# Three reorderings of an already tuned block: a subtraction moved ahead in the prologue, input transposes moved into an output projection, the first two tiles of a layer interleaved

## The chip, the cores and the metric

The kernel runs on one core of one Trainium2 chip. The metric is the device time of one execution in microseconds (us), lower is better. Names used here: PE is TensorE (PEld its weight loads), DVE is VectorE, ACT is ScalarE, POOL is GpSimd, SP is the engine that issues the transfers.

## The reference, cut to what matters

The reference computes one block on `x` of shape (4, 1024, 256). Each half begins with a layer norm without learned weights, scaled and shifted per batch by a small modulation product:

```python
h = _layernorm(x, axis=-1) * (1 + ca) + sa
x = x + ga * _L0_attn_ref(h, Wq, bq, Wk, bk, Wv, bv, Wo, bo)   # 16 heads of 64, causal, tanh projections
h = _layernorm(x, axis=-1) * (1 + cb) + sb
x = x + gb * _L0_ffn_ref(h, ...)                                # two layers

# attention
q, k, v = (tanh(states @ W + bias), split into heads)
ctx = softmax(causal(q @ k.T / 8)) @ v
return jnp.tanh(ctx @ Wo + bo)

# each of the two layers of the second half
h = shift_token(x); q, k, v = split(h @ wqkv)        # 8 heads of 64
q, k = rotary(l2norm(q) * qs, l2norm(k) * ksc)
x = x + local_attention(q, k, v) @ wo                # window 128
h = layernorm(shift_token(x)) * lg + lb
a, g = split(h @ w1 + b1); x = x + (a * gelu(g)) @ w2 + b2
```

## The kernel before, in words

Every engine has its own program, written by hand as a list of calls, with semaphores between them. So the order in which an engine does its work is the order of the lines; an engine that waits holds up all that is queued behind the waiting instruction. Matrix products are made from high and low parts (`three_products`, L71 to L76): an operand is split into a rounded high part by ACT (`stream_hi`) and a remainder by DVE (`stream_lo`), and three products are added up in PSUM. A projection of 512 columns is six matmuls (two halves of the 256 inputs by three products).

**Attention phase.** It runs batch after batch (four), and in a batch over eight pairs of heads. The input of a batch is normalised by DVE (`statistics`, `shifts`, `normalise_chunk`), transposed by PE (`stream_T`), split by `stream_hi` and `stream_lo`, all in two chunks of 512 tokens. For batches 0 and 1 this happens in the prologue; for batches 2 and 3 it happens at the end of batch 0 and of batch 1, beside the output projection. The one power on POOL (`inverse_deviations`, L269) gives the standard deviations.

In the prologue, PE makes six projections of the first pair (`PROJ`: values of chunk 0, values of chunk 1, queries 0, keys 0, queries 1, keys 1). A projection of chunk c waits for `stream_lo(0, c)`. ACT turns each into a full and a high part (`tanh_full` L517, `tanh_hi` L522), DVE subtracts them (`split_projection` L295); `tanh_full(i)` waits for `split_projection(i - 2)`, since there are two stage buffers. ACT's list is: projections 0, 1, 2, `stream_hi(1, 0)`, projections 3, 4, `stream_hi(1, 1)`, projection 5. Meanwhile POOL splits the output weights `wo` (L274 a cast, L276 a subtraction, 2048 elements a partition each), which the output projections need only at the end of the batch.

At a batch's end the output projection is made of four accumulations (c, m), chunk c of tokens by half m of the outputs, each of 24 matmuls over the eight pairs of heads. ACT applies tanh (L608), DVE the gate (`gate_attended` L469), PE transposes back (`output_T` L727), DVE adds to the residual (`add_attended` L476). PE's next batch begins with `scores(..., 1)`. PE, ACT and DVE each wait at the loop's top, or before it, for `n_lo`, which counts the finished `stream_lo`. For the third batch's end (and the fourth's) there is no later input to prepare.

**Layer phase.** Each of the two layers goes over 32 tiles of 128 tokens in a loop that is software pipelined by hand, and then over eight chunks of the feed-forward part. Ahead of the loop stands a start that takes tiles 0 and 1 and the transposes of tile 2 through their first steps. For a tile these are: POOL copies it (`stage_tile` L1105) and puts one carried column into the operand (`carry_in`, `carry_out`), PE transposes it (`stream_T` L1590), ACT and DVE split it, PE projects values, queries and keys (`project`, in the order 2, 0, 1), ACT squares queries and keys (`squares` L1215), DVE sums them (`squared_norms` L1377, L1379), POOL takes two powers (L1110, L1114), DVE rotates (`rotate_q`, `normalise_keys`, `rotate_k`), POOL adds the two halves of the rotation (`add_rotated` L1118), and PE transposes the result (`qk_T` L1613), which ACT (`copy_queries`) and DVE (`copy_keys`) copy out of PSUM. `qk_T(..., 0)` writes the same PSUM bank as `stream_T`, `qk_T(..., 1)` the same as the value projection. `carry_in` of tile t waits in POOL's list behind the powers of the tile before.

## Time and profile before

| | us |
|---|---|
| median of 3 runs (lowest to highest) | 2591.67 (2588.89 to 2592.57) |
| the profiled execution, its time | 2589.23 |
| its span in the trace | 2587.4 |
| PE busy in the span | 2381.7 |
| DVE / ACT / POOL busy | 1919.3 / 1543.3 / 618.5 |

The span is what the trace covers; 1.8 us lie around it. The mean granted clock of TensorE is 0.966 of full speed. A busy share is an average over stages with different limits, so the stages that the change touches have to be read one by one: the prologue (0 to 54 us), the ends of batches 0 and 1 (about 263 to 303 and 506 to 546 us) and the starts of the two layers (about 1062 to 1101 and 1814 to 1848 us).

### The profile page before, as it was taken

How to read it: one execution, taken by the hardware profiler on the slowest of the kernel's cores; microseconds unless marked ns; L12 is line 12 of the kernel's file. 1: busy time of each engine (PE TensorE's matmuls, PEld its weight loads, DVE VectorE, ACT ScalarE, POOL GpSimd, SP SyncE). 2: the span in 40 equal slices, each digit the busy share in tenths (PEclk: the TensorE clock that was granted, in tenths of full speed). 3: DMA queues.
4: the chain of work that ended last, by engine and by line, in shares of the span. 5: the costliest groups of instructions: out<-in, count | busy, mean ns of one | idle time of the engine just before them, and what ended most of it. 6: DMA issues, size and time to landing. Idle time of an engine off the chain costs nothing. (4 is left out here: it accounts for less than half of the span.)

```text
span 2587.4 us, 65680 instructions
## 1 busy us (share of the span) xinstructions
PE 2381.7 (92%) x21336; PEld 1898.6 (73%) x21336; DVE 1919.3 (74%) x4552; ACT 1543.3 (60%) x3026; POOL 618.5 (24%) x711
## 2 busy tenths in 40 slices
PE   5999899999999995299999998999799999998995
PEld 4767667767777774288888886888588888886884
DVE  6999699879969994567777776666477777765666
ACT  4777477667747773266666665344366666664442
POOL 1000000000000000444444444212344444442222
PEclk8999999999999998599999999999899999998998
DMA  3100100010001003100000000100100000001003
GB/s 110 39 18 12 56 19 12 29 46 16 15 6 52 12 18 113 64 1 0 8 0 8 1 8 3 48 0 0 45 0 7 1 8 0 8 0 51 0 0 130
DMA packets 70204, 62.43 MB, mean 24 GB/s; under 512 B 3972, under 2 KB 67196, under 8 KB 69760
## 3 DMA queue, kind: packets, MB, share of 16 engines
q1 hardware_dynamic: 70144, 61.66, 7.5%
q8 instruction: 34, 0.56, 0.1%
q14 instruction: 26, 0.21, 0.0%
HBM read 49.05 MB, written 8.40 MB: 22 GB/s over the span
## 5 line engine op out<-in xcount | busy, mean ns | idle before, releaser
L511 ACT ACTIVATE at_p<-at_ps_s,at_shift 128x1024 f32<-128x1024 f32 (+3 forms) x384 | 336.1, 900 | 85.6 <-PE at_ps_s L680 48.8
L311 DVE TENSOR_TENSOR at_p_lo<-at_p,at_p_hi 128x1024 f16<-128x1024 f32 (+3 forms) x384 | 357.2, 951 | 5.5
L1228 ACT ACTIVATE ly_probs<-ly_masked,ly_small,ly_rq 128x256 f32<-128x256 f32 x512 | 302.2, 592 | 40.0 <-DVE ly_small L1421 40.0
L1640 PEld LDWEIGHTS ly_ps<-ly_values,ly_probs_T 128*128 128x128 f32 x2048 | 248.3, 191 | 48.7 <-issue 48.7
L1640 PE MATMUL ly_ps<-ly_values,ly_probs_T 128*128 x2048 | 269.5, 274 | 12.6 <-ACT ly_probs_T L1236 12.6
L1418 DVE CUSTOM_DVE_ANT_0 ly_masked<-ly_ps,ly_mask 128x256 f32<-128x256 f32 x520 | 199.7, 421 | 91.5 <-PE ly_ps L1621 90.9
L1236 ACT ACTIVATE ly_probs_T<-ly_ps 128x512 f32<-128x512 f32 x256 | 151.9, 594 | 178.8 <-PE ly_ps L1630 131.2
L1118 POOL TENSOR_TENSOR ly_rope_a<-ly_rope_a,ly_rope_t 128x512 f32<-128x512 f32 x132 | 169.2, 1282 | 304.1 <-DVE ly_rope_t L1391 304.1
L708 PE MATMUL at_ps_o<-at_v,at_p_hi 128*128 128x65 f16 x2304 | 237.7, 193 | 0.0
L709 PE MATMUL at_ps_o<-at_v,at_p_hi 128*128 128x64 f16 x2304 | 236.8, 194 | 0.0
L708 PEld LDWEIGHTS at_ps_o<-at_v,at_p_hi 128*128 128x128 f16 x2304 | 210.6, 96 | 34.5 <-issue 25.7
L710 PE MATMUL at_ps_o<-at_v,at_p_lo 128*128 128x65 f16 x2304 | 235.7, 192 | 0.0
L306 DVE CAST at_p_hi<-at_p 128x1024 f16<-128x1024 f32 (+3 forms) x384 | 206.7, 556 | 30.0 <-ACT at_p L511 21.4
L1377 DVE TENSOR_REDUCE ly_norm<-ly_sq 128x8 f32<-128x512 f32 x136 | 93.3, 686 | 174.3 <-ACT ly_sq L1215 172.8
L710 PEld LDWEIGHTS at_ps_o<-at_v,at_p_lo 128*128 128x128 f16 x2304 | 212.3, 99 | 0.0
L709 PEld LDWEIGHTS at_ps_o<-at_v,at_p_hi 128*128 128x128 f16 x2304 | 212.0, 97 | 0.0
L74 PE MATMUL ly_ps<-ly_a_hi,ly_operands 128*128 128x512 f32 x408 | 181.1, 444 | 14.0 <-DVE ly_operands L1370 7.8
L74 PE MATMUL at_ps_m<-at_hT,at_w_hi 128*128 128x512 f32 (+1 forms) x396 | 175.3, 443 | 14.6 <-DVE at_hT L361 11.0
L517 ACT ACTIVATE at_stage<-at_ps_m,at_bias 128x512 f32<-128x512 f32 x198 | 136.0, 687 | 87.3 <-PE at_ps_m L76 84.1
L75 PE MATMUL ly_ps<-ly_a_lo,ly_operands 128*128 128x512 f32 x408 | 164.7, 404 | 0.0
L76 PE MATMUL ly_ps<-ly_a_hi,ly_operands 128*128 128x512 f32 x408 | 164.0, 402 | 0.0
L76 PE MATMUL at_ps_m<-at_hT,at_w_lo 128*128 128x512 f32 (+1 forms) x396 | 158.1, 399 | 0.0
(232 smaller groups left out, 6303.0 us busy)
## 6 DMA issues: line engine op xcount, KB each, us to landing
ly_a_raw<-in_ffn_wqkv SPq DMA_DIRECT2D x3, 1536.0 KB, 6.4
at_w_raw<-in_Wv SPq DMA_DIRECT2D x34, 128.0 KB, 2.2
at_w_raw<-in_Wq SPq DMA_DIRECT2D x34, 128.0 KB, 2.3
at_w_raw<-in_Wk SPq DMA_DIRECT2D x34, 128.0 KB, 2.3
at_xio<-in_states SPq DMA_DIRECT2D x4, 1024.0 KB, 6.0
x<-at_xio SPq DMA_DIRECT2D x4, 1024.0 KB, 4.4
stream<-x SPq DMA_DIRECT2D x4, 1024.0 KB, 9.6
out_x<-x SPq DMA_DIRECT2D x4, 1024.0 KB, 10.3
```

The source lines that it names most:

```text
L74: pe.matmul(out, w_hi, x_hi, start=first, stop=False, skip_group_check=True)
L76: return pe.matmul(out, w_lo, x_hi, start=False, stop=last, skip_group_check=True)
L306: dve.tensor_copy(p_hi[u % P_RING][:, :, off:], probs[u % P_RING][:, :, off:]).then_inc(p_hi_done, 1)
L311: dve.tensor_tensor(p_lo[u % P_RING][:, :, off:], probs[u % P_RING][:, :, off:], p_hi[u % P_RING][:, :, off:], ALU.subtract).then_inc(p_lo ...
L511: act.activation(probs[u % P_RING][:, :, off:], ps_s[u % 2][:, :, off:], ACT.Exp, bias=shift[:], scale=SCORE_SCALE).then_inc(exp_done, 1)
L708: pe.matmul(out, ph, ones_hi, start=(kt == 0 and t == 0), stop=False, skip_group_check=True)
L709: pe.matmul(out[:, 0:DH], ph, lo, start=False, stop=False, skip_group_check=True)
L710: step = pe.matmul(out, pl, ones_hi, start=False, stop=(kt == qc * CT + t), skip_group_check=True)
L1118: pool.tensor_tensor(ra[:, i, :], ra[:, i, :], rt[:, i, :], ALU.add).then_inc(s["add_done"], 1)
L1228: step = act.activation(pr[:, j % 2, h, :], sm[:, j % 2, h, :], ACT.Exp, bias=small[:, j % 2, 1, h:h + 1], scale=rq[:, par, 2 * j + h:2 * ...
L1418: dve.tensor_tensor_reduce(sm[:, j % 2, h, :], ps_s[h][:, half], mask[:, par].rearrange("p a b -> p (a b)"), 1.0, -3.0e38, ALU.add, ALU.ma ...
L1640: step = pe.matmul(ps_pv[:, cols], pT[:, (2 * slot + h) * P:(2 * slot + h + 1) * P], vv[:, v_slots[slot], cols], start=(j == 0 and h == 0 ...
```

## The change

Three parts, all of them orders of existing calls. One wait is added; no operation is added or removed.

```diff
                 inverse_deviations(1)
+                pool.wait_ge(n_xn, 2 * NC)
                 pool.wait_ge(ld_wo, 16)
                 pool.tensor_copy(wo_hi[:], xio[:]).then_inc(wo_done, 1)
...
                 stream_lo(0, 0)
+                stream_lo(0, 1)
                 shifts(1)
                 normalise_chunk(1, 0)
-                stream_lo(0, 1)
                 normalise_chunk(1, 1)
...
                     gate_attended(0, 0)
                     if b + 2 < B:
                         statistics(b + 2)
-                    gate_attended(0, 1)
-                    if b + 2 < B:
+                        gate_attended(0, 1)
                         shifts(b + 2)
                         normalise_chunk(b + 2, 0)
                         normalise_chunk(b + 2, 1)
-                    gate_attended(1, 0) if b + 2 >= B else None
-                    add_attended(0)
-                    if b + 2 < B:
+                        stream_lo(b + 2, 0)
                         gate_attended(1, 0)
-                        stream_lo(b + 2, 0)
+                        add_attended(0)
+                        stream_lo(b + 2, 1)
+                    else:
+                        gate_attended(0, 1)
+                        gate_attended(1, 0)
+                        add_attended(0)
                     gate_attended(1, 1)
                     add_attended(1)
-                    if b + 2 < B:
-                        stream_lo(b + 2, 1)
...
+                            if m == 1 and c == 0 and b + 2 < B:
+                                stream_hi(b + 2, 0)
                             if m == 0 and c == 1 and b + 2 < B:
-                                stream_hi(b + 2, 0)
+                                stream_hi(b + 2, 1)
                     if b + 2 < B:
-                        stream_hi(b + 2, 1)
                         act.wait_ge(n_lo, NC * (b + 3))
...
                             for hp in range(HP):
+                                if (c, m, hp) == (1, 0, HP // 2) and b + 2 < B:
+                                    stream_T(b + 2, 0)
...
                             if (c, m) in ((1, 0), (1, 1)):
                                 output_T(b, m)
-                            if c == 1 and b + 2 < B:
-                                stream_T(b + 2, m)
+                            if (c, m) == (1, 0) and b + 2 < B:
+                                stream_T(b + 2, 1)
...
+                    stage_tile(0, 0)
+                    carry_in(l, 0, 0, 0)
+                    stage_tile(1, 1)
                     pool.memset(on[:], 0.0).then_inc(s["on_zeroed"], 1)
-                    stage_tile(0, 0)
-                    stage_tile(1, 1)
                     pool.memset(kT[:, :, P:2 * P], 0.0).then_inc(s["kz_done"], 1)
-                    carry_in(l, 0, 0, 0)
                     carry_out(l, 0, 0, 0)
+                    carry_in(l, 1, 1, 1)
                     stage_tile(0, 2)
                     inverse_query_norms(l, 0, 0, LP)
                     inverse_key_norms(l, 0)
                     add_rotated(l, 0, 0)
-                    add_rotated(l, 0, 1)
-                    carry_in(l, 1, 1, 1)
                     carry_out(l, 1, 1, 1)
                     stage_tile(1, 3)
+                    add_rotated(l, 0, 1)
...
                     stream_hi(l, 0, 0)
+                    copy_values(l, 0, 0)
                     squares(l, 0, 0)
                     squares(l, 0, 1)
-                    copy_values(l, 0, 0)
+                    stream_hi(l, 1, 1)
+                    copy_values(l, 1, 1)
                     copy_queries(l, 0, 0)
-                    stream_hi(l, 1, 1)
                     squares(l, 1, 0)
                     squares(l, 1, 1)
-                    copy_values(l, 1, 1)
...
                     rotate_q(l, 0, 0)
+                    stream_lo(l, 1, 1)
                     normalise_keys(l, 0)
                     rotate_k(l, 0, 0)
+                    squared_norms(l, 1, 0)
                     copy_keys(l, 0, 0)
-                    stream_lo(l, 1, 1)
-                    squared_norms(l, 1, 0)
...
+                    stream_T(l, 1, 1)
+                    after(pe, "v_done", nth_projected(l, 0) + 1)
+                    project(l, 1, 1, 2)
                     qk_T(l, 0, 0)
-                    after(pe, "v_done", nth_projected(l, 0) + 1)
+                    project(l, 1, 1, 0)
+                    after(pe, "v_done", nth_projected(l, 1) + 1)
                     qk_T(l, 0, 1)
+                    project(l, 1, 1, 1)
                     after(pe, "qT_done", nth_rotated(l, 0) + 1)
+                    stream_T(l, 2, 0)
+                    hold(pe, s["tick"], (s["ld_wo"], 16 * l + 16))
+                    after(pe, "kz_done", l + 1)
                     after(pe, "kT_done", nth_rotated(l, 0) + 1)
-                    hold(pe, s["tick"], (s["ld_wo"], 16 * l + 16))
-                    stream_T(l, 1, 1)
-                    for i in (2, 0, 1):
-                        project(l, 1, 1, i)
-                    stream_T(l, 2, 0)
-                    after(pe, "kz_done", l + 1)
                     scores(l, 0, 0, 0)
```

In the rows that follow the lines of the changed kernel are shifted by 1 to 4 against those of the kernel before (L361 is L362 there, L354 is L355, L545 and L548 are L546 and L549, L608 is L609, L1590 is L1594, L1613 is L1617).

VectorE in the prologue, from the end of the statistics of batch 1. L361 is `stream_lo`, L354 `normalise_chunk`, L295 `split_projection`. Before:

```order
L89 SCALAR_TENSOR_TENSOR at_columns<-at_vtmp 128x8
L361 TENSOR_TENSOR at_hT<-at_first,at_hT 128x2x512
L345 SCALAR_TENSOR_TENSOR at_columns<-at_columns 128x8
L354 TENSOR_SCALAR at_first<-at_first,at_columns 128x256 x4
L361 TENSOR_TENSOR at_hT<-at_first,at_hT 128x2x512
L354 TENSOR_SCALAR at_first<-at_first,at_columns 128x256 x4
L295 TENSOR_TENSOR at_vT_lo<-at_stage,at_vT_hi 128x512 x2
L295 TENSOR_TENSOR at_q0lo<-at_stage,at_q0hi 128x512
```

After:

```order
L89 SCALAR_TENSOR_TENSOR at_columns<-at_vtmp 128x8
L362 TENSOR_TENSOR at_hT<-at_first,at_hT 128x2x512 x2
L346 SCALAR_TENSOR_TENSOR at_columns<-at_columns 128x8
L355 TENSOR_SCALAR at_first<-at_first,at_columns 128x256 x8
L296 TENSOR_TENSOR at_vT_lo<-at_stage,at_vT_hi 128x512 x2
L296 TENSOR_TENSOR at_q0lo<-at_stage,at_q0hi 128x512
L296 TENSOR_TENSOR at_k0lo<-at_stage,at_k0hi 128x512
L362 TENSOR_TENSOR at_hT<-at_first,at_hT 128x2x512
```

The second `stream_lo` has moved ahead of the shifts and both chunks of the norm of batch 1.

ScalarE at the end of batch 0 (and 1), with the semaphores that each instruction waits for. L608 is tanh, L545 and L548 are `stream_hi`. Before:

```order
L608 ACTIVATE at_y<-at_ps_s,at_bo 128x512 [waits at_yt_mm,at_op_mm]
L608 ACTIVATE at_y<-at_ps_s,at_bo 128x512 [waits at_op_mm]
L608 ACTIVATE at_y<-at_ps_o,at_bo 128x512 [waits at_yt_mm,at_op_mm]
L545 ACTIVATE at_p<-at_ps_m,modT 128x512 [waits at_pj_lo,n1_T,at_p_lo_done,at_pj_mm]
L545 ACTIVATE at_p<-at_ps_m,modT 128x512
L548 ACTIVATE at_hT<-at_ps_m,modT 128x512 x2
L608 ACTIVATE at_y<-at_ps_o,at_bo 128x512 [waits at_op_mm]
L545 ACTIVATE at_stage<-at_ps_m,modT 128x512 [waits at_pj_lo,n1_T,at_p_lo_done,at_pj_mm]
L545 ACTIVATE at_stage<-at_ps_m,modT 128x512
L548 ACTIVATE at_hT<-at_ps_m,modT 128x512 x2
```

After:

```order
L609 ACTIVATE at_y<-at_ps_s,at_bo 128x512 [waits at_yt_mm,at_op_mm]
L609 ACTIVATE at_y<-at_ps_s,at_bo 128x512 [waits at_op_mm]
L546 ACTIVATE at_p<-at_ps_m,modT 128x512 [waits at_pj_lo,n1_T,at_p_lo_done,at_pj_mm]
L546 ACTIVATE at_p<-at_ps_m,modT 128x512
L549 ACTIVATE at_hT<-at_ps_m,modT 128x512 x2
L609 ACTIVATE at_y<-at_ps_o,at_bo 128x512 [waits at_yt_mm,at_op_mm]
L546 ACTIVATE at_stage<-at_ps_m,modT 128x512 [waits at_pj_lo,n1_T,at_p_lo_done,at_pj_mm]
L546 ACTIVATE at_stage<-at_ps_m,modT 128x512
L549 ACTIVATE at_hT<-at_ps_m,modT 128x512 x2
L609 ACTIVATE at_y<-at_ps_o,at_bo 128x512 [waits at_op_mm]
```

Both `stream_hi` now stand one tanh earlier; the last tanh of the batch is ACT's last operation ahead of the loop.

TensorE at the start of a layer, after the three projections of tile 0. L1590 transposes a tile's input, L1613 the rotated queries or keys, L74 to L76 are half a projection. Before:

```order
L1613 MATMUL ly_ps<-ident,ly_rope_a 128x128 x4
L1004 ISA
L1004 REGISTER_ALU
L1613 MATMUL ly_ps<-ident,ly_rope_a 128x128 x4
L1004 REGISTER_ALU
L50 ISA
L1004 REGISTER_ALU
L1590 MATMUL ly_ps<-ident,ly_xs 128x128 x2
L1004 REGISTER_ALU
L74 MATMUL ly_ps<-ly_a_hi,ly_operands 128x512
L75 MATMUL ly_ps<-ly_a_lo,ly_operands 128x512
L76 MATMUL ly_ps<-ly_a_hi,ly_operands 128x512
```

After:

```order
L1594 MATMUL ly_ps<-ident,ly_xs 128x128 x2
L1008 ISA
L1008 REGISTER_ALU
L74 MATMUL ly_ps<-ly_a_hi,ly_operands 128x512
L75 MATMUL ly_ps<-ly_a_lo,ly_operands 128x512
L76 MATMUL ly_ps<-ly_a_hi,ly_operands 128x512
L74 MATMUL ly_ps<-ly_a_hi,ly_operands 128x512
L75 MATMUL ly_ps<-ly_a_lo,ly_operands 128x512
L76 MATMUL ly_ps<-ly_a_hi,ly_operands 128x512
L1008 ISA
L1617 MATMUL ly_ps<-ident,ly_rope_a 128x128 x4
L1008 ISA
```

The transposes and the value projection of tile 1 now stand ahead of the transposes of tile 0's rotated queries; the query and key projections follow between and behind those of tile 0's keys.

## Rows read from the trace of the kernel before

**Rows 1.** The page: clock in 40 slices; one group (busy, mean ns)
```profile
PEclk8999999999999998599999999999899999998998
...
L1377 DVE TENSOR_REDUCE ly_norm<-ly_sq 128x8 f32<-128x512 f32 x136 | 93.3, 686 | 174.3 <-ACT ly_sq L1215 172.8
```

**Rows 2.** Timeline of the prologue: start us, length us, operation [idle before]
```profile
22.10 1.48 ACT L548 ACTIVATE at_hT<-at_ps_s,modT 128x512 fp32r<-128x512 f32 x2
...
24.06 1.89 POOL L274 CAST at_wo_hi<-at_xio 128x2048 fp32r<-128x2048 f32 x1
26.03 4.50 POOL L276 TENSOR_TENSOR at_wo_lo<-at_xio,at_wo_hi 128x2048 fp32r<-128x2048 f32 x1
...
24.14 1.83 DVE L345 SCALAR_TENSOR_TENSOR at_columns<-at_columns 128x8 f32<-128x8 f32 x1 [1.53 <-POOL at_columns L269]
26.01 5.63 DVE L354 TENSOR_SCALAR at_first<-at_first,at_columns 128x256 f32<-128x256 f32 x4
...
32.83 0.79 PE L74 MATMUL at_ps_m<-at_hT,at_w_hi 128*128 128x512 f32 x1 [7.97 <-DVE at_hT L361]
...
43.02 0.73 ACT L517 ACTIVATE at_stage<-at_ps_m,at_bias 128x512 f32<-128x512 f32 x1
```

**Rows 3.** L1359 of VectorE (ns min/median/max), and POOL beside it
```profile
L1359 DVE TENSOR_TENSOR ly_rope<-ly_rope,ly_rows x4: 678/778/4977, 1056.1 to 1062.2; 128x512 f32<-128x512 f32 x4
...
1056.24 4.87 POOL L1089 TENSOR_TENSOR stream<-stream,modB 128x2048 f32<-128x2048 f32 x1 [2.23 <-DVE stream L1334]
```

**Rows 4.** Timeline at the end of the first batch
```profile
287.18 0.40 PE L76 MATMUL at_ps_o<-at_cT,at_wo_lo 128*128 128x512 f32 x1
289.81 1.04 PE L742 MATMUL at_ps_m<-ident,at_p 128*128 128x128 f32 x8
295.49 0.51 PE L680 MATMUL at_ps_s<-at_q0hi,at_k0hi 64*128 64x384 f16 x2 [4.64 <-DVE at_hT L361]
302.97 0.39 PE L680 MATMUL at_ps_s<-at_q0hi,at_k0hi 64*128 64x512 f16 x2
...
293.81 1.23 DVE L361 TENSOR_TENSOR at_hT<-at_stage,at_hT 128x1024 fp32r<-128x1024 f32 x1 [2.58 <-ACT at_hT L548]
```

**Rows 5.** Timeline of TensorE at the end of the third batch
```profile
772.45 0.40 PE L76 MATMUL at_ps_o<-at_cT,at_wo_lo 128*128 128x512 f32 x1
780.55 0.39 PE L680 MATMUL at_ps_s<-at_q0hi,at_k0hi 64*128 64x512 f16 x2
```

**Rows 6.** Timeline of TensorE at the end of the second batch
```profile
530.47 0.40 PE L76 MATMUL at_ps_o<-at_cT,at_wo_lo 128*128 128x512 f32 x1
545.80 0.39 PE L680 MATMUL at_ps_s<-at_q0hi,at_k0hi 64*128 64x512 f16 x2
```

**Rows 7.** Windows after two restarts: length, busy by engine, clock, DMA
```profile
core 0: us, PE busy (x) PEld busy (x) DVE busy (x) ACT busy (x) POOL busy (x), PEclk, DMA share, GB/s
295.40:299.60 4.20, 4.11 (x16) 2.30 (x18) 2.39 (x3) 1.95 (x2) 0.00 (x0) 0.50 0.59 161
1089.60:1095.40 5.80, 5.72 (x14) 4.52 (x15) 0.02 (x1) 0.03 (x1) 0.52 (x2) 0.50 0.00 0
```

**Rows 8.** Timeline at the start of the first layer, TensorE and GpSimd
```profile
1076.62 0.39 PE L76 MATMUL ly_ps<-ly_a_hi,ly_operands 128*128 128x512 f32 x1
1082.62 1.11 PE L1613 MATMUL ly_ps<-ident,ly_rope_a 128*128 128x128 f32 x4 [5.61 <-POOL ly_rope_a L1118]
1089.68 0.80 PE L74 MATMUL ly_ps<-ly_a_hi,ly_operands 128*128 128x512 f32 x1 [1.31 <-DVE ly_operands L1370]
1100.78 0.47 PE L74 MATMUL ly_ps<-ly_a_hi,ly_operands 128*128 128x512 f32 x1 [2.15 <-POOL ly_operands L1098]
...
1079.69 1.64 POOL L1114 TENSOR_TENSOR ly_rk<-ly_norm,ly_expo 128x8 f32<-128x8 f32 x1
1081.29 1.27 POOL L1118 TENSOR_TENSOR ly_rope_a<-ly_rope_a,ly_rope_t 128x512 f32<-128x512 f32 x1
```

**Rows 9.** Timeline of GpSimd at the start of the second layer
```profile
1814.15 0.53 POOL L1143 MEMSET ly_on<- 128x512 f32 x1 [12.62 <-DVE stream L1577]
```

## The prediction

> **What bounds the kernel now.** I read the page first. PE is busy 92% of the span, so time can only be found where PE stands still or runs at half its clock. The row of the granted clock has an 8 in slice 1, a 5 in slice 17 and a few lone 8s [rows 1]: a start, the seam between the two phases, and restarts after pauses. The timelines of the four stretches that the change touches then say who is late there.
>
> Prologue: PE stands 7.97 us, from 24.86 to 32.83, and is released by DVE's `stream_lo(0, 1)` (L361) [rows 2]. That subtraction had its input at 23.58, when ACT's high part of chunk 1 ended (22.10 + 1.48). It came late because of DVE's list: ahead of it stood a shift, issued at 24.14, that took 1.83 us for 8 columns, and four scalings that took 5.63 us. POOL ran its cast from 24.06 for 1.89 us and its subtraction from 26.03 for 4.50 us in the same time [rows 2].
>
> End of batch 0: PE finishes the last output projection at 287.58 (287.18 + 0.40), makes the two groups of transposes, and then stands 4.64 us until 295.49, released by DVE's `stream_lo` at 293.81 + 1.23 [rows 4]. The granted clock is then 0.50, that is 1.2 GHz, from 295.4 to 299.6 [rows 7]. Batch 1 ends alike [rows 6].
>
> Layer start: after the key projection of tile 0 (1076.62 + 0.39) PE stands 5.61 us until POOL has added the rotated query, then goes from pause to pause, and projects tile 1 from 1089.68 on [rows 8] at a granted clock of 0.50 [rows 7]. The loop's first projection starts at 1100.78, released by POOL's carried column [rows 8].
>
> **Part 1, the prologue.** DVE is idle at 23.6, so `stream_lo(0, 1)` runs at 23.65 and takes 1.23 us (L361's time in [rows 4]): it ends at 24.9, 0.04 us after PE's first projection. PE goes on at about 24.95 where it had gone on at 32.83: 7.9 us earlier. The moved work of POOL does not vanish. Its new wait is for both chunks of batch 1's norm; undisturbed, these eight scalings and the shift take about 2.9 us (DVE has done them by 27.8), and POOL then runs 1.89 + 4.50 us. What is under it now? DVE's `split_projection`, with two SBUF operands. [rows 3] show such an operation (L1359, two SBUF operands, 0.68 us at the least) taking 4.98 us beside a POOL subtraction of 4.87 us: it was shut out for all of it. So DVE gets a split in at 27.8, POOL casts from 28.5 to 30.4, a second split gets in, POOL subtracts from 31.05 to 35.5, and the third split ends at 36.2. ACT wants it for `tanh_full(4)`: that tanh started at 43.02 before [rows 2] and starts at 36.3 now. Gain 6.7 us. Without the exclusion it would start at 34.2, right behind ACT's other work, gain 8.8; if POOL gets its two operations in back to back, about 37.0, gain 6.0. I take 6.7, since DVE's request is queued while POOL waits for its own semaphore. Nobody needs the output weights before 262 us.
>
> The Trainium skill, page SBUF — State Buffer, section Who interferes with whom, says that a VectorE instruction with two SBUF inputs contends with a GpSimd instruction that reads SBUF, and that the loser is blocked for the whole instruction. It speaks against a part of this edit, and by that rule the trace agrees (4.98 beside 4.87); a reading in which only the scalings are shut out would make the sum 2.1 us better.
>
> **Part 2, two batch ends.** The third batch's end has no input to prepare, so it shows what PE does when nobody has to be waited for: from the end of its last output matmul (772.45 + 0.40) to the first scores of unit 4 (780.55) it takes 7.70 us [rows 5]. At batch 0 the same way takes 302.97 - 287.58 = 15.39 us [rows 4], at batch 1 545.80 - 530.87 = 14.93 us [rows 6]. After the change ACT's and DVE's work on the input lies inside the fourth accumulation: ACT takes chunk 0 from 278.5 (its norm is done at 277.4) to 281.4, chunk 1 from 283.1 to 285.9, DVE subtracts until 287.1, and PE's last matmul ends only at 288.6. So the way becomes 7.70 us at both. What is added ahead: the second eight transposes now come before the last accumulation. Eight take at most 1.04 us [rows 4], and the first eight wait some 0.1 us for the norm; 1.0 us together. Gains: 15.39 - 7.70 - 1.0 = 6.7 and 14.93 - 7.70 - 1.0 = 6.2, sum 12.9 us. In it is the half clock after the restart: the third batch shows none after a shorter pause. If it came all the same, only the pause is won, about 4.2 us each, 8.4 in all. Ends for the range: 8.4 and 14. The transfers for the next batch move with DVE's last addition, and wait for nothing new.
>
> **Part 3, two layer starts.** The chain of the first, worked with the durations of the trace. Key projection of tile 0 ends at 1077.0; tile 1's transposes follow at once; ACT's two copies wait for its second square and end at 1078.3; DVE's stand behind the rotation of the query and end at 1080.6. PE pauses 3.2 us (5.61 before) and runs tile 1's value projection at the low clock (six matmuls at 0.43) until 1083.3. The rotated query is ready at 1081.29 + 1.27 = 1082.56 [rows 8], so its transposes follow without a wait, to 1084.3; the query projection to 1086.3 (half at each clock), the key transposes to 1087.0, the key projection to 1088.4, and the scores start at 1088.7 (1096.9 before). ACT's last square ends at 1089.1, DVE's sum (0.69 [rows 1] and a floor of 0.17) at 1090.0, POOL's power of 1.64 [rows 8] at 1091.7, its copied column at 1091.9. The loop's first projection starts at 1092.0 against 1100.78 [rows 8]: 8.8 us; by DVE's mask copy I get 8.3. I take 8.5. The second layer has the same chain, and POOL's memset of 0.53 us [rows 9], which stood ahead of the first copy with PE waiting, now stands behind: 9.0. Sum 17.5 us. Bounds: at the low clock all through, the query and key projections and transposes cost 2.2 us more a layer: 13. With the high clock at once, 20. The second tile's sum of squares stands ahead of `copy_keys` on DVE, and PE's scores wait for that; I have it at 1088.7, level with PE.
>
> **Sum.** 6.7 + 12.9 + 17.5 = 37.1 us. Against the profiled execution, 2589.23 (span 2587.4, 1.8 around it), that gives 2552.1; it lies 2.4 below the median of the runs, against which I predict: 2591.67 - 37.1 = 2554.6, rounded 2554.5. The loops behind the changed places are fixed lists with PE at the bound, so nothing there gives the time back: from the first unit 4 of a batch to its output projection PE takes the same time after a slow restart and after a quick one.
>
> **Rivals.**
> - *The clock stays low longer* (25%). All starts and joins keep their pauses below 3.2 us, yet the clock of a restart is a matter of what came before. For it: each of the two restarts in [rows 7] ran at 0.50. Against: none at the third batch. Price: 12.9 falls to 8.4, 17.5 to 13: gain 28, 2563.5.
> - *The interleaving is serial in disguise* (6%). Each tile 1 step waits on DVE or ACT behind a tile 0 step and the pair takes as long as one after the other but for the first pause: part 3 gives 2 x 2.4 = 5 us, the sum 24.5, 2567. Against: PE's pauses there are POOL's two powers and two additions, in which DVE and ACT have room.
> - *More than forecast* (7%): no exclusion in the prologue (+2.1), high clock early (+2.5): gain 42, 2549.5.
> - *Edits that don't do what they say* (2%): another release stands right behind each one removed, and the time is the same, 2591.
> - *Slower* (3%): PE's clock. One mechanism: the changed pattern of pauses at a loop's entry leaves the granted clock at 0.50 for a long stretch instead of 4 to 6 us. A projection's matmul costs 0.43 for 0.23 us there, so in a PE-bound stretch every 10 us become some 18. It would eat 37 us after about 45 us of loop at the low clock, and decides from there; at 60 us of it the time is 2603. Against it: all 40 slices but the seam show 0.8 or more [rows 1].
>
> **How the numbers follow.** The forecast has 57%, with an own range of 2550 to 2559. The range for 8 in 10 goes from 2548.5, the better rival and run to run differences, to 2565, past the low clock rival and just short of the serial one. A measurement of this kernel tells 0.2%, 5 us, from no change. Faster by over 0.2%: all cases but the last two, 95%; within 0.2%: 2%; slower: 3%.
>
> **What the changed profile would show.** In the prologue no pause of PE above 1 us between 23 and 27, POOL's cast starting near 28, and a split of DVE taking 4 us or a pause of ACT near 34 to 36. At 287 to 296, PE's pause of 4.64 gone, 1.3 us before the last transposes, granted clock 1.00. At the layer starts a pause of about 3 us, then work, and some 25 us from the first transposes to the loop's first projection instead of 33.5. The prediction is wrong if the scores of the layer start wait for DVE's `copy_keys` by more than 1 us, if the last `stream_lo` of a batch ends after PE's last transposes, or if DVE's splits hold PE below the third projection of the prologue.

## The result, and the profile after

The changed kernel takes 2549.94 us (median of 4 runs, 2548.80 to 2553.85) where the kernel before takes 2592.12 (4 runs beside it, 2588.89 to 2593.90): ratio 0.9841, 95% interval 0.9824 to 0.9858. That is 42.2 us between medians. Measured again with the experiments, with 9 runs of before, it took 2551.32, 38.6 us less. The profiled execution of the change took 2553.85 us (span 2552.0), 35.4 less than that of before. Forecast were 37.1. The executions of before lie in two groups by PE's mean granted clock: of the 18 measured with the experiments, seven with 0.964 or 0.965 took 2591.55 to 2592.53 us, eleven with 0.966 to 0.969 took 2587.63 to 2590.83, so a median of before, and the difference taken from it, moves by up to some 2 us with how many of each group are among its runs.

The page of the changed kernel, its first two parts (columns as in [rows 1]):

```profile
PE 2372.6 (93%) x21336; PEld 1892.8 (74%) x21336; DVE 1917.2 (75%) x4552; ACT 1542.6 (60%) x3026; POOL 618.1 (24%) x711
...
PEclk9999999999999997699999998999999999998997
```

Slice 1 has a 9 where [rows 1] have an 8; the low figures at the seam between the phases are still there, the 57 us in which PE waits for the norm and the weights.

Both timelines, read at the same instructions, give the account of the 35.4 us (start times in us; the last column is what each stretch added). A batch's loop begins with scores of 384 columns; "unit 4" is its first one with scores of 512 columns, a few us later:

| start of | before | after | earlier by | of it new |
|---|---|---|---|---|
| the first scores of attention's loop | 54.15 | 47.80 | 6.35 | 6.35 |
| the scores of unit 4 behind batch 0 | 302.97 | 290.02 | 12.95 | 6.60 |
| the same behind batch 1 | 545.80 | 526.72 | 19.08 | 6.13 |
| layer 0, first transposes | 1067.30 | 1048.40 | 18.90 | -0.18 |
| layer 0, the loop's first projection | 1100.78 | 1072.68 | 28.10 | 9.20 |
| layer 0, first transposes of probabilities | 1105.61 | 1075.87 | 29.74 | 1.64 |
| layer 1, first transposes | 1815.1 | 1785.2 | 29.9 | 0.2 |
| layer 1, the loop's first projection | 1848.14 | 1809.20 | 38.94 | 9.0 |
| layer 1, first transposes of probabilities | 1851.33 | 1814.07 | 37.26 | -1.7 |
| the last output product of layer 1 | 2558.7 | 2520.4 | 38.3 | 1.0 |
| the end of the span | 2587.4 | 2552.0 | 35.4 | -2.9 |

The timeline of the changed kernel in the prologue, engine by engine (lines are shifted by the edits: `stream_lo` L362, shift L346, scalings L355, `split_projection` L296, POOL's cast L275 and subtraction L277, `tanh_full` L518). These answer to [rows 2]:

```profile
23.73 1.23 DVE L362 TENSOR_TENSOR at_hT<-at_first,at_hT 128x1024 fp32r<-128x1024 f32 x1 [0.99 <-ACT at_hT L549]
24.87 0.16 DVE L346 SCALAR_TENSOR_TENSOR at_columns<-at_columns 128x8 f32<-128x8 f32 x1
25.07 2.67 DVE L355 TENSOR_SCALAR at_first<-at_first,at_columns 128x256 f32<-128x256 f32 x8
27.65 0.68 DVE L296 TENSOR_TENSOR at_vT_lo<-at_stage,at_vT_hi 128x512 f16<-128x512 f32 x1
...
31.44 4.20 DVE L296 TENSOR_TENSOR at_q0lo<-at_stage,at_q0hi 128x512 f16<-128x512 f32 x1 [0.80 <-ACT at_q0hi L523]
...
27.80 2.29 POOL L275 CAST at_wo_hi<-at_xio 128x2048 fp32r<-128x2048 f32 x1 [3.57 <-DVE at_first L355]
30.17 4.92 POOL L277 TENSOR_TENSOR at_wo_lo<-at_xio,at_wo_hi 128x2048 fp32r<-128x2048 f32 x1
...
34.51 0.72 ACT L523 ACTIVATE at_k0hi<-at_ps_m,at_bias 128x512 f16<-128x512 f32 x1
35.74 0.69 ACT L518 ACTIVATE at_stage<-at_ps_m,at_bias 128x512 f32<-128x512 f32 x1 [0.51 <-issue]
```

DVE's second low part starts 0.04 us behind ACT's high part (which ends at 23.69), and the shift behind it takes 0.16 us where it took 1.83. The third split is the price: it was issued at 31.44, while POOL subtracted from 30.17 to 35.09, and ended at 35.64. `tanh_full(4)`, the full part of the fifth projection, starts 0.10 us behind it, 7.3 us earlier than before. (The profile names no releaser there; by the program this tanh waits for that split.)

PE at the end of batch 0 in the changed kernel, to be held against [rows 4]: there is no pause of 4.64 us in front of the first scores, and no matmul at the low clock behind them (0.34 us for the scores of 384 columns; 0.51 in [rows 4]). DVE's last low part ends at 280.91, ahead of PE's last transposes.

```profile
283.62 1.09 PE L729 MATMUL at_ps_o<-ident,at_y 128*128 128x128 f32 x8 [1.30 <-DVE at_y L470]
284.65 0.34 PE L682 MATMUL at_ps_s<-at_q0hi,at_k0hi 64*128 64x384 f16 x2
...
290.02 0.39 PE L682 MATMUL at_ps_s<-at_q0hi,at_k0hi 64*128 64x512 f16 x2
...
279.69 1.22 DVE L362 TENSOR_TENSOR at_hT<-at_stage,at_hT 128x1024 fp32r<-128x1024 f32 x1 [1.40 <-ACT at_hT L549]
```

And PE at the start of the first layer, the rows that answer to [rows 8], with matmuls of one kind left out:

```profile
1058.00 0.38 PE L1594 MATMUL ly_ps<-ident,ly_xs 128*128 128x128 f32 x2
1061.67 0.50 PE L74 MATMUL ly_ps<-ly_a_hi,ly_operands 128*128 128x512 f32 x1 [3.29 <-DVE ly_operands L1374]
...
1063.44 1.11 PE L1617 MATMUL ly_ps<-ident,ly_rope_a 128*128 128x128 f32 x4
1064.21 0.78 PE L74 MATMUL ly_ps<-ly_a_hi,ly_operands 128*128 128x512 f32 x1
...
1069.56 1.13 PE L1625 MATMUL ly_ps<-ly_operands_plain 64*128 64x256 f32 x8 [0.64 <-DVE ly_operands_plain L1412]
...
1072.68 0.47 PE L74 MATMUL ly_ps<-ly_a_hi,ly_operands 128*128 128x512 f32 x1 [1.40 <-POOL ly_operands L1102]
...
1074.15 1.89 PE L1656 MATMUL ly_ps<-ly_operands_plain 128*128 128x256 f32 x8
```

The pauses of PE behind tile 1's transposes are 3.29, 0.64 and 1.40 us, where [rows 8] begin with 5.61; from the first transposes to the loop's first projection it is 24.3 us, where it was 33.5. The last row is the eight output products behind that projection. In the kernel before the same eight took 3.56 us in the first layer and 1.89 in the second; in the changed kernel it is 1.89 in the first and, in the timeline of PE in the second layer:

```profile
1809.20 0.47 PE L74 MATMUL ly_ps<-ly_a_hi,ly_operands 128*128 128x512 f32 x1 [2.11 <-POOL ly_operands L1102]
...
1810.77 3.46 PE L1656 MATMUL ly_ps<-ly_operands_plain 128*128 128x256 f32 x8
```

PE's clock is at its low level there (granted clock 0.51 from 1811 to 1814). So the two rows of 1.64 and -1.7 us in the table are one thing: which of the two loop entries runs at the low clock.

### The profile page after: what moved, and what is told of

Same layout as the page of the kernel before. It is cut to its first block and busy times, and to the rows that moved or that the text cites. A ratio compares the mean times of both kernels' runs of the same rounds, so it can differ in the third digit from the quotient of the medians.

```text
span 2552.0 us, 65683 instructions
## 1 busy us (share of the span) xinstructions
PE 2372.6 (93%) x21336; PEld 1892.8 (74%) x21336; DVE 1917.2 (75%) x4552; ACT 1542.6 (60%) x3026; POOL 618.1 (24%) x711
## 5 line engine op out<-in xcount | busy, mean ns | idle before, releaser
L74 PE MATMUL ly_ps<-ly_a_hi,ly_operands 128*128 128x512 f32 x408 | 179.7, 440 | 17.2 <-DVE ly_operands L1374 11.8
L518 ACT ACTIVATE at_stage<-at_ps_m,at_bias 128x512 f32<-128x512 f32 x198 | 135.7, 685 | 77.8 <-PE at_ps_m L76 73.3
L74 PE MATMUL at_ps_m<-at_hT,at_w_hi 128*128 128x512 f32 (+1 forms) x396 | 174.5, 441 | 6.6 <-DVE at_hT L362 3.0
L76 PE MATMUL ly_ps<-ly_a_hi,ly_operands 128*128 128x512 f32 x408 | 162.8, 399 | 0.0
L1118 POOL TENSOR_TENSOR ly_rk<-ly_norm,ly_expo 128x8 f32<-128x8 f32 x68 | 111.4, 1638 | 193.0 <-DVE ly_norm L1383 192.8
```

What stands on the lines that cost most here:

```text
L74: pe.matmul(out, w_hi, x_hi, start=first, stop=False, skip_group_check=True)
```

## The experiments

Times are medians, compared with the kernel before as measured beside them. Twelve kernels were run; one of them is the changed kernel once more.

**The three parts, each alone on the kernel before.** `pro_only` has the edits of the prologue (DVE's list and POOL's wait), `ends_only` those of the batch ends, `layers_only` those of the layer starts, each word for word as in the diff. `order_only` has of the prologue only the first of its two edits:

```diff
                 stream_lo(0, 0)
+                stream_lo(0, 1)
                 shifts(1)
                 normalise_chunk(1, 0)
-                stream_lo(0, 1)
                 normalise_chunk(1, 1)
```

Expected of `pro_only`: 

> The prologue part alone on the kernel before: DVE's second low part first, POOL's output-weight split behind the norm. In the profile of the change tanh_full(4) stood 7.3 us earlier and the first scores of the loop 6.35 us earlier. My theory: 6.35 us less, 2585.8 against a median of 2592.1, and nothing of it given back by the loop. Rival (the loop gives back what the start wins, since its first iteration waits for DVE's mask and weight work anyway): under 2 us. In the last stage of the kernel, where POOL's addition and DVE's addition start within 0.3 us of each other, I expect the time from the last output product to the end to be either near 28.6 (DVE first, as in the profile of before) or near 31.5 us (POOL first, as in the profile of the change), whatever the edit.

Expected of `order_only`: 

> Of the prologue part only DVE's order; POOL's wait for the norm is left out, so its cast runs from 24.06 and its subtraction from 26.03 to 30.53, as in the kernel before. My theory: the shift and the eight scalings are shut out until POOL has subtracted and end near 33.2, the three splits stand behind them, tanh_full(2) waits for the first of them (33.9) and tanh_full(4) starts near 39.4, against 43.02 before and 35.74 in the change: gain 2.7 us. Rival (POOL's work costs DVE nothing that anyone waits for, the order alone is the gain): 6.3 us, as pro_only.

Expected of `ends_only`: 

> The batch ends alone. The profile of the change has 6.61 and 6.13 us less there: theory 12.7 us less, 2579.4, PE without a pause of more than 1.5 us and at full clock behind both ends. Rival (the transfers and weight loads of the next batch, or a low clock in the next batch's first iteration, give part back): 8 to 10 us.

Expected of `layers_only`: 

> The layer starts alone. The profile of the change has the loop's first projection 9.2 and 9.0 us earlier, but the first transposes of the probabilities 10.8 and 7.3 us earlier, with PE's first output product of the loop at full clock in one layer and at half in the other. Theory: 18.2 us less for both, with 1.6 us more or less per layer according to PE's clock at the loop's entry: 15 to 21.5. Rival (part of the gain seen belongs to the earlier parts, which shift when the layer phase starts): under 14 us.

Measured, beside 2590.58 us for the kernel before (18 runs):

| kernel | us | ratio, 95% interval | less by |
|---|---|---|---|
| pro_only | 2583.41 | 0.9972, 0.9962 to 0.9983 | 7.2 |
| order_only | 2587.59 | 0.9985, 0.9976 to 0.9994 | 3.0 |
| ends_only | 2579.05 | 0.9954, 0.9941 to 0.9968 | 11.5 |
| layers_only | 2571.47 | 0.9929, 0.9915 to 0.9943 | 19.1 |

The three parts add up to 37.8 us, the whole gave 38.6 and 42.2: they do not hinder one another. The rivals of a loop that gives the prologue's gain back and of layer starts worth under 14 us are out by the medians. Ends worth 8 to 10 us are not out by the medians alone, whose interval goes from 8.3 to 15.3 us; the profile decides that. From the loop's first scores to the first scores behind batch 2's end `ends_only` takes 708.27 us (55.77 to 764.04), the kernel before 721.02 (54.15 to 775.17), 12.75 less.

`order_only` tells what POOL's wait is for. DVE and POOL in its prologue:

```profile
24.91 1.85 DVE L345 SCALAR_TENSOR_TENSOR at_columns<-at_columns 128x8 f32<-128x8 f32 x1
26.80 6.98 DVE L354 TENSOR_SCALAR at_first<-at_first,at_columns 128x256 f32<-128x256 f32 x8
...
24.22 2.52 POOL L274 CAST at_wo_hi<-at_xio 128x2048 fp32r<-128x2048 f32 x1
26.82 4.55 POOL L276 TENSOR_TENSOR at_wo_lo<-at_xio,at_wo_hi 128x2048 fp32r<-128x2048 f32 x1
...
34.49 0.69 ACT L517 ACTIVATE at_stage<-at_ps_m,at_bias 128x512 f32<-128x512 f32 x1 [4.71 <-DVE at_vT_lo L295]
```

The shift takes 1.85 us for 0.16 and ends 0.02 us behind POOL's cast; the scalings take 6.98 for 2.67, the difference is POOL's subtraction. ACT then waits 4.71 us for the first split, and `tanh_full(4)` starts at 39.44 (expected 39.4). So `pro_only`'s gain has two shares: the order brings 3.0 us, the wait on top of it 4.2 more (the ranges of the two kernels, 2584.70 to 2588.67 and 2582.01 to 2584.25 us, do not touch). The wait alone, in the old order, was not run. POOL's subtraction shuts DVE out once in either kernel; what the wait changes is which instruction is shut out, eight scalings that all else stands behind, or a split that is nearly early enough.

**The restart of PE.** `restart_late`, on the changed kernel, has both groups of input transposes behind the third output projection:

```diff
-                                if (c, m, hp) == (1, 0, HP // 2) and b + 2 < B:
-                                    stream_T(b + 2, 0)
...
                             if (c, m) == (1, 0) and b + 2 < B:
+                                stream_T(b + 2, 0)
                                 stream_T(b + 2, 1)
```

Expected: 

> The changed kernel with both groups of input transposes behind the third output projection, where the first group stood inside it. ACT needs 2.8 us for the high part of chunk 0 before the second group may overwrite the tile, so PE stands about 2.9 us there, in front of its fourth output projection, at both batch ends; what follows the projection is as in the change. Theory (PE's pauses there are simple waits and the clock keeps its level over one of 2.9 us, as at the layer starts it did for the first 1.2 us behind 3.29): 5.8 us more than the changed kernel, 2556 to 2557. Rival (the clock falls behind every pause of this length and costs another 1.5 to 2 us each): 9 to 10 us more.

Measured: 2559.52 us, 8.2 more than the changed kernel's 2551.32 and 9.6 more than its 2549.94. The theory's 5.8 is out, the rival is right in kind. Its PE timeline behind the first batch, and the windows of that stretch (PEclk is the column behind the engines):

```profile
278.47 1.94 PE L744 MATMUL at_ps_m<-ident,at_p 128*128 128x128 f32 x8 [3.08 <-ACT at_hT L549]
280.06 0.78 PE L74 MATMUL at_ps_o<-at_cT,at_wo_hi 128*128 128x512 f32 x1
...
284.05 0.52 PE L74 MATMUL at_ps_o<-at_cT,at_wo_hi 128*128 128x512 f32 x1
...
290.16 0.34 PE L682 MATMUL at_ps_s<-at_q0hi,at_k0hi 64*128 64x384 f16 x2
```

```profile
278.40:281.00 2.60, 2.53 (x10) 2.44 (x11) 2.60 (x3) 0.95 (x2) 0.00 (x0) 0.50 0.03 6
281.00:284.00 3.00, 3.00 (x8) 2.32 (x7) 0.73 (x2) 2.35 (x4) 0.00 (x0) 0.50 0.00 0
```

Behind a pause of 3.08 us PE ran at half its clock for 5.6 us: from the loop's first scores to the first scores of batch 1 it takes 242.65 us (47.51 to 290.16) against 236.88 in `after_again`, 5.77 more, of which the pause is 3.1 and the clock 2.7. Batch 1's end costs 5.7 in the same way. Of these 11.5 us 9.6 are left at the end of the profiled execution, since among others its first layer takes 1.2 us less, 0.9 of them at its start; between medians it is the 8.2. So nearly half of what the placement of the first group inside the projection gives, under running matmuls, is clock. That is not the share in the whole part: of the 12.7 us of the batch ends 3.6 lie behind the first scores of the next batch, where the kernel before takes 7.48 and 6.92 us to unit 4, partly at the low clock, and the change 5.37 and 5.39.

**PE's pause at a layer's start.** `lo_first`, on the changed kernel, gives DVE's low part of tile 1 first:

```diff
+                    stream_lo(l, 1, 1)
                     rotate_q(l, 0, 0)
-                    stream_lo(l, 1, 1)
```

Expected: 

> The changed kernel with DVE's low part of the layer's second tile ahead of the rotation of the first tile's query, where PE had waited 3.29 us for it. Theory (PE's first pause at a layer's start is cover: POOL's two powers and its addition, 58.89 to 63.39, set when the query's transposes can start, and PE and POOL were level there): the pause shrinks to about 2.1 us and one of about 1.1 us opens in front of the query's transposes; the loop's first projection comes at the same time, 0 us, but for what PE's clock does (up to 1.7 us a layer either way). Rival (PE's pause is on the path): 1.1 us less a layer, 2.2 in all.

Measured: 2552.79 us (2551.58 to 2556.85), no gain against 2549.94 and 2551.32. PE in the first layer:

```profile
1060.86 0.50 PE L74 MATMUL ly_ps<-ly_a_hi,ly_operands 128*128 128x512 f32 x1 [2.06 <-DVE ly_operands L1374]
...
1063.83 0.66 PE L1617 MATMUL ly_ps<-ident,ly_rope_a 128*128 128x128 f32 x4 [1.32 <-POOL ly_rope_a L1122]
...
1072.74 0.47 PE L74 MATMUL ly_ps<-ly_a_hi,ly_operands 128*128 128x512 f32 x1 [2.12 <-POOL ly_operands L1102]
```

The pause of 3.29 us became 2.06 and 1.32, and the loop's first projection comes 24.0 us behind the first transposes (24.3 and 24.5 in the two profiles of the change). In the second layer it is 22.9 for 24.0, but that us was won ahead of the edit's place, where PE's clock rose earlier. Counted from POOL's first power (1059.29 and 1797.53), behind that stretch, the projection comes 13.45 and 13.42 us later, where `after_again` has 13.86 and 13.44. So PE's pause is cover for POOL's two powers and its addition, as the theory said, and not on the path.

**The column behind POOL's last power.** `carry_first`, on the changed kernel:

```diff
-                    inverse_key_norms(l, 1)
                     carry_in(l, 2, 0, 2)
+                    inverse_key_norms(l, 1)
```

Expected: 

> The changed kernel with POOL's copied column for the third tile ahead of its last power. The loop's first projection waited 1.40 and 2.11 us for that column behind a power of 1.64. Theory: it starts 1.4 and 2.1 us earlier, of which some 1.0 a layer reaches the transposes of the probabilities, since ACT's exponentials end at 74.9 in the change's first layer and PE is there at 75.9: 2 us less in all, give or take 1.7 per layer for PE's clock. Rival (the exponentials wait for the power, which is now behind a copy, and PE only waits in another place): within 0.5 us of the changed kernel.

Measured: 2548.50 us (2546.24 to 2549.40), 2.8 less than the changed kernel beside it (2549.08 to 2552.14; the ranges overlap by 0.3). Its profile shows more: from the first transposes to the first transposes of the probabilities 25.7 us in both layers, against 27.7 and 28.9 in `after_again`. The direction is that of my theory, the size is not: 5.1 us in the profile where I had 2, of which 4.3 are left at its end. PE in its second layer:

```profile
1805.66 0.48 PE L74 MATMUL ly_ps<-ly_a_hi,ly_operands 128*128 128x512 f32 x1
...
1807.14 1.89 PE L1656 MATMUL ly_ps<-ly_operands_plain 128*128 128x256 f32 x8
```

There is no pause in front of the projection, and the eight output products take 1.89 us, at full clock now in both layers. About 1.6 of the 3.2 us in this layer are the clock; the projection itself comes 1.5 us earlier here and 1.9 in the first layer, where 2.1 and 1.4 were expected.

**The prologue behind its second projection.** `hi_late`, on the changed kernel, puts ACT's high part of batch 1's second chunk behind the sixth tanh:

```diff
-                    elif i == 4:
-                        stream_hi(1, 1)
+                stream_hi(1, 1)
                 split_weights(1)
```

Expected: 

> The changed kernel with ACT's high part of batch 1's second chunk behind the sixth tanh of the prologue instead of behind the fifth. In the change's profile PE stands 4.00 us until ACT's sixth tanh at 40.1, and 2.77 us of ACT's copies lie ahead of it. Theory (behind the third projection the prologue is bound by ACT's chain and no longer by DVE): the values' transposes start at 38.2 instead of 40.94, but the first scores have to wait for those copies until 41.0 (42.73 in the change), so the loop's first scores come at 46.0 instead of 47.8: 1.8 us less. Rival (the third split, shut out until 35.64, is what the prologue waits for): it would still start tanh_full(4) at 35.7, and moving work that lies behind it gives under 0.5 us.

Measured: 2549.48 us (2546.51 to 2552.47), 1.8 less than beside it but with the ranges across each other. PE in its prologue:

```profile
38.05 0.61 PE L652 MATMUL at_ps_m<-at_ident,at_vT_hi 128*128 128x128 f16 x8 [2.42 <-issue]
...
40.77 0.61 PE L681 MATMUL at_ps_s<-at_q0hi,at_k0hi 64*128 64x512 f16 x2 [1.67 <-ACT at_hT L549]
...
42.49 4.54 PE L778 MATMUL at_ps_o<-at_first 128*4 128x512 f32 x8
46.97 0.34 PE L681 MATMUL at_ps_s<-at_q0hi,at_k0hi 64*128 64x384 f16 x2
```

The values' transposes and the first scores come where the theory had them (38.05, and 40.77 for 42.73), so ACT's chain was the bound. But the eight products behind them take 4.54 us (granted clock 0.50 from 42.5 to 45), where `after_again` has 3.69 for them from 44.31 on. Half of the gain is left at the loop's start, and PE's clock in the first layer's start takes 1.3 us of it back in this profile. The gain in time is not shown.

**The last stage.** The additions of the residual are shared, batch 1 on POOL and the others on DVE. `after_again` is the changed kernel once more; `tail_dve` has `POOL_BATCHES = ()`, all on DVE; `tail_mix` has that, and the first addition ahead of the fourth multiplication:

```diff
-POOL_BATCHES = (1,)
+POOL_BATCHES = ()
...
                     dve.tensor_tensor(part, part, gb, ALU.mult).then_inc(gated, 1)
+                    if b == 2:
+                        dve.wait_ge(gated, 1)
+                        dve.wait_ge(ld[0], 16)
+                        first = h[:, 0:TB, :]
+                        dve.tensor_tensor(first, first, x1[:, 0:TB, :], ALU.add).then_inc(added, 1)
```

Expected of `after_again`: 

> The changed kernel once more, as the measure for the three beside it. Both theories: 2550 us within 2; if the last stage (28.7 us with DVE first, 31.6 with POOL first, in five profiles so far) is what made its profiled execution 4 us longer than its others, this profile shows 28.7 and a time near 2550, or 31.6 and a time near 2553.

Expected of `tail_dve`: 

> The changed kernel with all four additions of the last stage on DVE, none on POOL. Theory: the first batch's addition on DVE takes 2.3 us instead of being shut out for POOL's 4.68 us, so its store goes out at the same place as where DVE came first, and the four stores (14 to 15.4 us from the first one to the end) set the end: 28 to 28.7 us from the last output product in every execution, 0 to 3 us less than the changed kernel, about 1.5 between medians. Rival (DVE's fourth addition, 2.3 us more of it, comes last and the second engine was worth its place): 1 to 2 us more.

Expected of `tail_mix`: 

> The changed kernel with all four additions of the last stage on DVE and the first of them ahead of the fourth multiplication. Theory (the four stores, 4 MB, set the end from the moment when the first goes out): batch 0's store goes out 2.2 us earlier, and the stage takes 26 us from the last output product where all four additions on DVE behind the multiplications took 28.2: 2 to 2.5 us less than that kernel's 2550.0. Rival (the stores wait for the last addition, which comes no earlier): no change against it.

Measured: 2551.32, 2549.99 and 2549.20 us (2549.08 to 2552.14, 2549.37 to 2550.86, 2548.07 to 2550.65), so between medians no gain of either edit is shown; what follows is read from the profiles. The end of the changed kernel in its first profiled execution, and the row of the DMA engines' busy tenths from 2520 to 2552:

```profile
2531.11 4.68 POOL L880 TENSOR_TENSOR stream<-stream,out_x 128x2048 f32<-128x2048 f32 x1 [21.36 <-DMA out_x<-x]
2531.36 10.98 DVE L872 TENSOR_TENSOR stream<-stream,out_x 128x2048 f32<-128x2048 f32 x3
2537.97 5.57 SPq L857 DMA_DIRECT2D out<-stream  x4
...
DMA  1000679999999999999930039999999999999990
```

The same of `after_again`:

```profile
2531.77 2.28 DVE L872 TENSOR_TENSOR stream<-stream,out_x 128x2048 f32<-128x2048 f32 x1
2532.23 6.17 POOL L880 TENSOR_TENSOR stream<-stream,out_x 128x2048 f32<-128x2048 f32 x1 [22.09 <-DMA out_x<-x]
2534.08 9.07 SPq L857 DMA_DIRECT2D out<-stream  x4
...
DMA  0000097999999999999999999999999999980000
```

This is the same program in two executions. In one POOL's addition starts 0.25 us ahead of DVE's, DVE is shut out, the first store goes out at 2537.97 and the DMA engines stand for some 2 us between loads and stores. In the other DVE is 0.46 us ahead, and the first store goes out at 2534.08. From the last output product to the end it is 31.6 us or 28.7. Of the eleven profiles of kernels with POOL's addition, that of before among them, nine have DVE first and 28.6 to 28.9 us, two (the change's first and `ends_only`) have POOL first and 31.6. With DVE alone (`tail_dve`) it is 28.2, and the five runs lie within 1.5 us. Both `tail_mix`'s theory and its rival were off: it takes 27.7 us in that profile, 0.5 less and not 2. The DMA engines carry 8.39 MB in this stage and are busy from the first load to the last store, so it seems that an earlier store only queues behind the loads; no run shows that by itself.

**Together.** `best` has `carry_first`, `tail_mix` and `hi_late` on the changed kernel.

Expected: 

> The changed kernel with three edits at once: the third tile's column ahead of POOL's last power (profile: 5.2 us less over the two layer starts), the last stage's additions on DVE with the first ahead of the fourth multiplication (2.5 us expected), and the high part of batch 1's second chunk behind the sixth tanh (0.95 us earlier at the loop's start, given back at the layer's start by PE's clock). Theory: 2550.5 - 4 to 5 - 2.5 = 2543.5 to 2544, with 0 to 1 from the last. Rival (a start that moves by 1 us changes where PE's clock rises and falls in the layer starts, and the gain of the first edit, half of which is clock, is lost): 2547.

Measured: 2546.07 us (5 runs, 2544.97 to 2547.20), ratio to before 0.9830 (0.9817 to 0.9843). All five lie below all nine runs of the changed kernel (median 2550.07, from 2548.80), by 4.0 us between medians. That is between my two figures; the profile has 25.0 and 25.6 us from first transposes to the probabilities' (27.7 and 28.9), and 28.6 in the last stage, so of `tail_mix` nothing is left here but that the last stage no longer depends on which engine comes first.

## Why the prediction was right

The number (2554.5) is 4.6 us above the median first measured and 3.2 above the second; the range holds both, while the forecast's own range, from 2550, just misses the first. The rival *more than forecast* had 2549.5, nearer to that median, but its conditions are not what the profiles show: the exclusion was there, and the layer starts gave 18.2 us and not 20. Step by step:

**Prologue, 6.7 forecast.** Measured 6.35 at the loop's first scores, 7.2 between medians for the part alone. The mechanism was as described: no pause of PE between 23 and 27, POOL's cast at 27.80, a split held for 4.20 us (4.98 beside 4.87 in [rows 3] was the row it was costed from), `tanh_full(4)` at 35.74 for the forecast 36.3. Wrong was the price of the exclusion, 2.1 us: ACT had its other work until 35.23 (forecast 34.2), so the split was waited for by 0.51 us only, by 1.05 in the profile of `pro_only` and by 1.61 in that of `hi_late`, where ACT came sooner. The gain at the tanh was 7.3 us; about 1 was lost behind it, 0.7 of it as the eight products ahead of the loop took 3.42 us at a granted clock of 0.80 (2.74 before, at 1.00). That is no effect of the edits: with the prologue of before, `ends_only` has 3.93 us for these eight and `layers_only` 3.01. The first scores come at 54.15, 54.97 and 55.77 us in the three profiles with the old prologue and at 46.92 to 48.11 in the eight with the new one, 7.4 us apart in the mean, which is nearer to the 7.2 between medians than the 6.35 of the first pair. The Trainium skill, page SBUF — State Buffer, section Who interferes with whom, says that a VectorE instruction with two SBUF inputs contends with a GpSimd instruction that reads SBUF, and that whoever comes second is blocked for the whole instruction. The trace agrees: the split was issued 1.27 us into a POOL subtraction and ended 0.55 us behind it. The page adds that forms with a scalar can contend too, in modes that use both ports; the scalings of `order_only`, with one tensor input each, are held for 4.3 us.

**Batch ends, 12.9 forecast.** Measured 6.60 + 6.13 = 12.7, and 12.75 for the part alone inside one execution. The working by the third batch's end held. The clock's share in it, priced at 4.5 us (12.9 - 8.4), measured 3.6. `restart_late` shows the other bound at work: with a pause of 3.08 us left, 5.8 us a batch are lost in its profile, 2.7 of them to the clock.

**Layer starts, 17.5 forecast.** Measured at the loop's first projection 9.2 and 9.0 for 8.8 (8.5 taken) and 9.0. The pause was 3.29 for 3.2, the scores waited 0.64 us for `copy_keys`, under the 1 us named. Two details were off: tile 1's value projection ran mostly at full clock, the query projection at the low one, where I had the low clock first and half of each behind; the two errors cancel. And the term ended too early: it was summed to the loop's first projection, while PE's clock differs also behind it, 1.6 us for and 1.7 against in the two layers.

**The sum against the time.** 37.1 forecast, 35.4 between the profiled executions: +0.2 from the terms, summed to the loops' first projections (6.35 + 12.73 + 18.2 = 37.3), nothing in sum by the clock behind these (1.6 - 1.7), +1.0 in the long stretches between, -2.9 from the order of POOL and DVE in the last stage, which no edit touches. That the end is so near is in part luck: without the 2.9 us of the last stage it would be 38.3. Between medians it is 38.6 to 42.2. The terms were read from one execution of before, 2589.23 us; three of the four executions beside the 42.2 took 2591.67 us and more. Where the rest of the 42.2 lies, between executions that have no profile, stays open.

Of the rivals, *the clock stays low longer* shows itself in `restart_late`, but the change's pauses avoid it at the batch ends. *Serial in disguise* is out by the layer starts' 18.2 us, and *slower* by the clock's row and the time.

## What to carry to other kernels

Ask of a pause not only how long it is but what it leaves behind: here one of 3.1 us cost 5.8, and 3.6 of the 12.7 us that the batch ends gave were clock. When a small engine's long instruction cannot be avoided, choose under which instruction of the other engine it falls; the same POOL subtraction held DVE's scalings for 4.3 us, with ACT waiting 4.7 us behind them, and cost ACT 0.5 to 1.6 us beside a split. And an end of a kernel at which two engines that shut each other out start within 0.5 us of each other can differ by 3 us from run to run: look for it before a gain of a few microseconds is put down to an edit.

## What the runs showed of the hardware

- Size is no protection: a DVE shift of 8 columns took 1.85 us for 0.16 beside a POOL cast, and ended with it. In the last stage the exclusion works both ways: POOL's addition takes 4.68 us if it is first, and 6.17 if DVE is 0.46 us ahead.
- With its own work the same, POOL's addition of 128x2048 takes over twice as long as DVE's (4.68 and 2.28 us); since each shuts the other out, sharing the additions made the last stage no faster than DVE alone (28.7 and 28.2 us).
- PE's clock can fall in the middle of a stretch without a pause of its own: in the first layer's start it restarts at full clock behind 3.29 us (0.39 us a matmul from 1062.0) and is at the low level 2 us later (1.11 us for four transposes, 0.78 for a matmul), and back near 1066. In `lo_first`, with two shorter pauses in the same place, it stayed full there and was low at the loop's entry instead (3.14 us for the eight output products that take 1.89 at full clock). The total over both layers was the same to 0.1 us, by accident: the low clock cost 1.2 us more at the first loop's entry, and 1.1 were won in the second layer before the edit's place. Why it falls in one place and not in the other the runs do not tell.
